# A vision state-space block with attention: the low half of the projected rows, formed by TensorE in the bank and copied by ScalarE

## The reference

```
x_hw = xc.reshape(Bsz, D, L)                       # D = 192, L = 64*64
x_wh = xc.transpose(0, 1, 3, 2).reshape(Bsz, D, L)
xs = stack([x_hw, x_wh, x_hw[..., ::-1], x_wh[..., ::-1]])   # 4 directions
x_dbl = einsum('kcd,bkdl->bkcl', x_proj_w, xs)     # 20 rows a direction
dts, Bv, Cv = split(x_dbl, [12, 16])
dt = softplus(einsum('kdr,bkrl->bkdl', dt_proj_w, dts) + dt_proj_b)
h = exp(dt * A) * h + dt * Bv * u                  # at each of 4096 positions, 4 states
y = einsum('bkdn,bkn->bkd', h, Cv)
```

## Time and profile before

| | |
|---|---|
| median of 3 runs | 10451.7 us (10447.28 to 10456.88) |
| the profiled execution, own time | 10460.32 us |
| its span | 10458.4 us |
| TensorE busy | 9132.7 us (87%) |
| VectorE busy | 7813.8 us (75%) |
| ScalarE busy | 6224.0 us (60%) |
| GpSimd busy | 3667.5 us (35%) |
| mean granted TensorE clock | 0.94 |

### The profile page before, as it was taken

The page is one execution under the profiler, slowest core; times in us unless marked ns, Lnnn a source line. Parts: engine busy times, 40 slices in busy tenths (PEclk is TensorE's granted clock), DMA queues, the critical chain, the costliest instruction groups (busy, mean ns, idle before and its releaser), DMA issues.

```text
span 10458.4 us, 108398 instructions
## 1 busy us (share of the span) xinstructions
PE 9132.7 (87%) x27904; PEld 4899.5 (47%) x27904; DVE 7813.8 (75%) x9039; ACT 6224.0 (60%) x7683; POOL 3667.5 (35%) x1920
## 2 busy tenths in 40 slices
PE   5999959999599995999959999699996999969999
PEld 2336723367233662336623366233662336623366
DVE  6977669866698666976669776697666976669776
ACT  4755647556475554755557555575555755557555
POOL 3850038500385003850048500485004850048500
PEclk8999979999799997999979999799997999979999
DMA  1320013200132001320013200132001320013200
GB/s 43 109 71 5 8 38 109 72 5 8 40 108 72 5 8 44 105 70 5 8 44 109 66 7 6 44 109 67 6 6 44 110 67 5 7 45 109 67 5 8
DMA packets 158736, 487.41 MB, mean 47 GB/s; under 512 B 21177, under 2 KB 21785, under 8 KB 125486
## 3 DMA queue, kind: packets, MB, share of 16 engines
q1 hardware_dynamic: 158254, 482.04, 14.6%
HBM read 454.69 MB, written 27.26 MB: 46 GB/s over the span
## 4 chain that ended last, share of the span: by engine, by line
PE 59%; issue 16%; DVE 15%; POOL 4%; ACT 3%; DVEq 1%; DMA 0%; ACTq 0%; SPq 0%; POOLq 0%
DVE h L1039 6%; PE ps L509 5%; PE ps L522 5%; PE ps L510 5%; PE ps L524 5%; PE ps L523 5%; PE ps L511 5%; PE ps L432 4%; PE ps L355 3%; PE ps L393 2%; PE ps L390 2%; PE ps L377 2%; PE ps L374 2%; PE ps L347 2%; PE ps L348 2%
## 5 line engine op out<-in xcount | busy, mean ns | idle before, releaser
L1164 DVE TENSOR_TENSOR pl<-pf,ph 128x1024 fp32r<-128x1024 f32 x1024 | 1254.7, 1225 | 1205.2 <-ACT ph L823 1204.1
L1039 DVE TENSOR_TENSOR_SCAN h<-ps,h,dbu 128x512 f32<-128x512 f32 x1536 | 1884.4, 1268 | 17.7 <-DVE h L1065 5.2
L897 POOL TENSOR_TENSOR dbu<-bs,du 128x1024 f32<-128x1024 f32 x768 | 1799.8, 2373 | 52.8 <-POOL du L888 52.8
L823 ACT ACTIVATE ph<-pf 128x1024 fp32r<-128x1024 f32 x1024 | 1085.3, 1060 | 833.5 <-PE ps L524 833.3
L842 POOL MEMSET xb<- 64x1024 f32 x16 | 15.2, 947 | 4280.2 <-issue 4276.5
L815 ACT ACTIVATE pf<-ps 128x1024 f32<-128x1024 f32 x1024 | 1051.0, 1026 | 644.6 <-PE ps L511 644.6
L697 ACT ACTIVATE ps<-dt,negA 128x512 f32<-128x512 f32 x1536 | 1032.6, 683 | 440.4 <-DVE h L1039 406.3
L1148 DVE TENSOR_REDUCE mx<-ps 128x1 f32<-128x512 f32 x1792 | 1164.8, 683 | 68.7 <-PE ps L432 42.2
L1047 DVE TENSOR_TENSOR hc<-h,ps 128x1024 f32<-128x1024 f32 x768 | 937.8, 1221 | 194.3 <-PE ps L366 114.5
L888 POOL TENSOR_TENSOR du<-dt,u 128x512 f32<-128x512 f32 x512 | 707.5, 1404 | 625.8 <-DVE dt L1029 625.8
L522 PE MATMUL ps<-ph,gth 128*97 128x512 f32 x2048 | 817.7, 399 | 80.8 <-ACT yraw L803 72.1
(11 more groups left out here) (175 smaller groups left out, 15899.1 us busy)
## 6 DMA issues: line engine op xcount, KB each, us to landing
bs<-rows SPq DMA_DIRECT2D x256, 1024.0 KB, 5.1
bs<-rows SPq DMA_DIRECT2D x512, 256.0 KB, 6.1
xa<-in_x SPq DMA_DIRECT2D x128, 256.0 KB, 2.9
xb<-in_x SPq DMA_DIRECT2D x128, 128.0 KB, 3.0
out<-fa SPq DMA_DIRECT2D x64, 256.0 KB, 2.0
out<-fa SPq DMA_DIRECT2D x64, 128.0 KB, 2.3
rows<-xd SPq DMA_DIRECT2D x256, 8.0 KB
gate<-in_sel SPq DMA_DIRECT2D x1, 384.0 KB
```

The source lines that it names most:

```text
L823: A(ph[:, mp % 2, :, :], pf[:, mp % 2, :, :], ACT.Copy).then_inc(S["ph_ready"], 1)
L897: pool.tensor_tensor(dbu[:, q, :, :], bs[par][:, q, :, :], du[:, r:r + 1, :].to_broadcast([P, 2, T]), ALU.mult).then_inc(S["dbu_ready"], 1)
L1039: dve.tensor_tensor_scan(h[:, j, ::step], ps[:, 2 + e, ::step], dbu[:, q, e, ::step], h[:, j, end:end + 1], ALU.mult, ALU.add)\
L1164: TT(pl[:, mp % 2, :, :], pf[:, mp % 2, :, :], ph[:, mp % 2, :, :].bitcast(F32), ALU.subtract)\
```

## The change

VectorE's `low_half` goes. TensorE gets `less_high`: a product of `minus` (minus the identity in rows 0 to 31, columns 32 to 63, zero elsewhere) with `xhl`, in fp32r, added onto bank 0 without clearing it. So partitions 32 to 63 of bank 0 then hold the rows minus their rounded value. ScalarE gets `copy_low`, which copies these 32 partitions to `xhl` and raises `xlo_ready`. `minus` is set up once, by a memset on GpSimd and one small VectorE instruction.

```
+                def less_high(par, g):
+                    pe.wait_ge(S["xhi_ready"], g + 1)
+                    mm(ps[:, 0, :], minus[:, :], xhl[par][:, :], start=False, stop=True, skip_group_check=True)\
+                        .then_inc(S["low_ready"], 1)
...
# TensorE, body
                     spread(2, par, g)
                     sum_second(g)
+                    if after:
+                        less_high(par, g + 2)
                     if nxt:
                         spread(0, 1 - par, g + 1)
# TensorE, ahead of the chunks
                 dtproj(0, g_0)
+                less_high(0, g_0)
                 spread(0, 0, g_0)
                 xdbl(0, 1, g_0 + 1)
                 dtproj(0, g_0 + 1)
+                less_high(1, g_0 + 1)
...
+                def copy_low(par, g):
+                    act.wait_ge(S["low_ready"], g + 1)
+                    A(xhl[par][LO:2 * LO, :], ps[LO:2 * LO, 0, :], ACT.Copy).then_inc(S["xlo_ready"], 1)
...
# ScalarE, body
                         soft_log(par, g + 2)
+                        copy_low(par, g + 2)
# ScalarE, ahead of the chunks
                 copy_high(0, g_0)
+                copy_low(0, g_0)
                 soft_abs(g_0)
...
                 soft_log(1, g_0 + 1)
+                copy_low(1, g_0 + 1)
...
+            TS(minus[0:LO, LO:2 * LO], eye[0:LO, 0:LO], -1.0, None, ALU.mult)
...
-                def low_half(par, g):
-                    dve.wait_ge(S["xhi_ready"], g + 1)
-                    TT(xhl[par][LO:LO + 32, :], ps[LO:LO + 32, 0, :], xhl[par][LO:LO + 32, :].bitcast(F32),
-                       ALU.subtract).then_inc(S["xlo_ready"], 1)
...
# VectorE, body
                     if after:
-                        low_half(par, g + 2)
                         residue(g + 2)
```

More of the change, by code:

```diff
@@ L88, in build @@
         eye1 = sb("eye1", [P, P])
+        minus = sb("minus", [P, P], F32R)
         avg = sb("avg", [P, P])
@@ L185, in build @@
             "conv_link", "conv_ready", "cs_ready", "u_ready",
-            "xdbl_ready", "xd_ready", "xhi_ready", "xlo_ready", "dtpre_ready", "soft_ready", "res_ready", "sp_ready",
+            "xdbl_ready", "xd_ready", "xhi_ready", "low_ready", "xlo_ready", "dtpre_ready", "soft_ready", "res_ready", "sp_ready",
             "dt_ready", "du_ready", "dA_ready", "rows_saved", "b_loaded0", "b_loaded1", "cbc_ready", "dbu_ready", "scan_link",
@@ L260, in _ @@
         def _(sp):
-            sp.wait_ge(S["pads_set"], 10)
+            sp.wait_ge(S["pads_set"], 11)
             for dst, src in LOADS:
@@ L832, in _ @@
         def _(pool):
-            for t in (win1[:, :], wo1[:, :], wa1[:, :], wx0[:, :], wx1[:, :], wdt[:, :], foldw[:, :], skip1[:, :], eye1[:, :], selr[:, :].bitcast(F32)):
+            for t in (win1[:, :], wo1[:, :], wa1[:, :], wx0[:, :], wx1[:, :], wdt[:, :], foldw[:, :], skip1[:, :], eye1[:, :], selr[:, :].bitcast(F32), minus[:, :].bitcast(F32)):
                 pool.memset(t, 0.0).then_inc(S["pads_set"], 1)
@@ L1013, in _ @@
                 dve.sem_inc(S["scan_set"], 1)
[L1015 to L1018, removed]
                 def residue(g):
@@ L1068, in _ @@
                 g_0 = b * G
-                low_half(0, g_0)
                 residue(g_0)
                 softplus(0, g_0)
-                low_half(1, g_0 + 1)
                 residue(g_0 + 1)
```

## The result

The changed kernel takes 10562.03 us in the median of 4 runs (10560.89 to 10562.93), the kernel before 10451.52 (10447.28 to 10456.88, 4 runs): a ratio of 1.0105 with an interval of 1.0088 to 1.0123. It is slower by 110.5 us where 77 was forecast; 10562 lies 8 us above the range. The profiled executions took 10562.34 and 10460.32, a difference of 102.0.

A forecast was written before the change was run, and what follows sets the result against it. VectorE bounds row-order chunks (97% busy); column-order ones are a cycle of 13.2 us TensorE and a 2.18 VectorE tail. Terms 7.65 + 0.7 + 0.95 + 0.35 = 9.65 us an item, 77 for 8: 10529, range 10498 to 10554.

The forecast's parts named there:

- Moved, and this decides: the release of the x projection: Column order: copy_low stands behind ScalarE's soft_one and log, so the x projection comes at 405.41 for 404.54: +0.87 a chunk.
- The product on TensorE is hidden: Added product behind sum_second: 0.44 us at most, done by about 404.5, before copy_low can start at 404.79.
- The mixture of gains and losses by kind of chunk: Chunks 1 to 5 -1.65 us, 6 to 8 +1.80, 9 to 13 +4.35, 14 to 16 -0.51, 17 to 28 +3.66.
- step 3: Mixed chunks with plain x projection: 14 and 15 at 14.57 us, 16 at 14.12; stretch 43.77 to 43.26.
- Step 1: Column order on ScalarE: copy_low starts 0.95 us behind the log's start, at 404.79, and ends at 405.37.
- Step 2: TensorE's granted clock: 1.00, the upper level of 2.4 GHz, in all five stretches, so no term hangs on it.
- the price of the strided products: TensorE: a product with strided moving side costs 1.96 - 1.12 = 0.84 us more; two in a column-order x projection.
- The ends: Outside chunks 1 to 28, per item: +0.7 us ahead of the chunks, +0.95 in chunk 0, +0.35 after the last x projection.
- The step from profile to median: Whole kernel: profiled execution 10460.3 lies 8.6 us above the median 10451.7, so 10537 becomes 10529.
- (a): Rival: copy hidden, VectorE's time comes back; row-order chunks 13.65 us, column-order 15.38, total 10371; chance 0.05.
- (b): Rival: column-order chunks lose less, 15.72 us by the second way round, +0.34 for +0.87; total 10485; chance 0.10.
- (c): Rival: ScalarE's copy costs more; 0.33 over the price gives 10603, the decay's price (+0.11) 10554; chance 0.10.

The follow-up runs named there:

- the release alone: Kernel before, low_half kept on VectorE, but the x projection released by a one-element ScalarE instruction behind the log: 10487.4 us, ratio 1.0037.
- ScalarE's time alone: Kernel before plus one unrelated 32 x 512 ScalarE copy that nothing waits for, behind the log: 10503.98 us, ratio 1.0049.
- the kernel with products twice: Changed kernel with each product of spread(0) issued twice, while TensorE waits for the copy: 10560.75 us, ratio 1.0104 against the kernel before.
- the kernel over 64 rows: Changed kernel with copy_low writing partitions 0 to 63 in place of 32 to 63: 10534.39 us, ratio 1.0079 against the kernel before.
- the spare copies: Kernel before plus an unrelated ScalarE copy from partition 64: 32 rows behind the log 10503.98 us, behind add_y0 10455.46; 64 rows behind add_y0 10451.56.

## Why the prediction was right in direction and too small

**The mechanism held.** "Moved, and this decides: the release of the x projection": the release alone costs a column-order chunk 0.47 (15.85), ScalarE's time alone nothing (15.38), and putting product and copy early gives 15.44. The product on TensorE is hidden, with 0.61 to spare. The copy itself takes 0.59 (0.58 taken) and holds ScalarE 0.50 (0.48 taken). The mixture of gains and losses by kind of chunk came as forecast, once the copy begins at partition 0, but for chunks 14 to 16 (step 3).

**Step 1 that failed: "log 403.84, `copy_low` 403.84 + 0.95".** It assumed that the copy overlaps the log's end as the 64-row copy in the earlier trace rows overlaps its neighbours. A copy that begins at partition 32 doesn't: 1.07. That is 0.12 a chunk, and 0.23 in chunks 14 to 16, where `add_y0` is late as well: 3.9 us in the first item, from the kernel with products twice (425.18) to the kernel over 64 rows without its two falls (423.28 - 2.04 = 421.24). The run over 64 rows gave back 27.6 us in all. The Trainium skill, "ScalarE: Activation LUTs", What ACT_TABLE_LOAD costs, gives an overlap of about 93 ns for instructions back to back and names no exception; the run over 64 rows agrees (1.05 - 0.95 = 0.10), the changed kernel doesn't (-0.02).

**Step 2: "The granted clock is 1.00 in all five ... so no term below hangs on it".** True of the kernel before, and a wrong inference. The change itself puts 0.45 to 1.10 us of idle time in one piece ahead of each x projection, and the clock falls for 3.4 us, three or four times a scan: 2.1 us in the first item by the run that keeps TensorE busy. That the idle time brings the falls is shown by this run, in which shorter waits leave one fall in eight scans, and by the release alone, whose waits are 0.46 and less from chunk 2 on and which has none. What the falls cost the whole kernel no run shows: without them the total was the same (10560.75).

**Step 3: chunks 14 to 16 at 14.57, 14.57 and 14.12.** These were worked out from the cycle through `copy_low` only. `add_y0` behind the copy was named as waiting, and priced after the last x projection alone. Here it ends a second cycle. In chunk 14 of the changed kernel it runs from 443.57 to 444.63 (above), and then:

```profile
444.68 1.97 PE L397 MATMUL ps<-pad,eye 128*128 128x512 f32 x2 [0.29 <-ACT pad L717]
```

TensorE waits another 0.29, behind the 0.77 already lost. Chunks 14 and 15 took 15.21, chunk 16 14.70. The kernel with the copy's start mended still has 44.43 in this stretch, 1.2 over the forecast. There chunk 14 takes 14.98 for 14.57: 0.19 is this second wait, and 0.22 comes from the price of the strided products. The forecast took off 2 x 0.84 = 1.68 where the x projection is plain, but TensorE's busy time in these chunks is less by 1.46 only, in the kernel before as in the changed one.

The three make 3.9 + 2.1 + 1.2 = 7.2 us in the first item, and the other stretches, without falls and with the copy's start mended, came 0.5 below the forecast: 6.7, which is 427.27 - 420.57.

**The ends.** The forecast had +2.0 an item outside the stretches. From the first x projection to that of chunk 1 it was +0.50 in the mean (+1.06 in the first item) for 1.65: the start takes 27.85 for 25.05, and chunk 0 13.33 for 15.63. In the other stages, where nothing was changed, an item takes 1.9 us less in the mean (802.0 for 804.5 in the first). With +13.8 from the first to the last scan instruction and +0.9 ahead of them, 13.8 + 0.9 - 1.9 = 12.8, and 102.0 / 8 = 12.75. The other stages take 798.7 to 805.9 over all kernels run, and this goes with the clock: they are at the lower level for 128.9 us of an item in the mean in the kernel before, 124.8 in the changed one and 128.2 with the products twice, for 111.5 where they are shortest and for 142.1 where they are longest. Why the clock there differs is open.

**The step from profile to median.** The forecast took off 8.6 us, as the profiled execution before lay that far above its median. The changed kernel's lies 0.3 above. So 25 us of the miss are in the sum, and 8 in this step.

**The rivals.** (a), the copy hidden: not here; but VectorE's time does come back in row order once the copy stands behind the first decay (13.78 for the 13.65 of this rival). (b): no column-order chunk comes near 15.72; `copy_high` still waits for `spread(2)`. (c), the copy costs more: its lower value, 10554, is nearest to the result, and 0.12 is nearly its +0.11, but by a late start and not by a longer copy. That (c)'s number is near is luck. The range stopped at this one dearer copy, with no room for what idle time on the bounding engine brings besides, and that went the same way.

**Two sums of the prediction.** (b)'s own terms, nine chunks at 0.53 and four at 0.4, make 6.4 us an item and not 5 to 6, so 10478 in place of 10485. The terms of chunk 0 give 244.01 - 243.04 = 0.97 for 0.95. Neither moves the forecast by more than 0.2 us.

## What to carry to other kernels

Work that is taken off a busy engine gains only where that engine is the bound, and its new place decides what it costs: put it behind whatever the bound waits for, and look at every instruction queued after it, not only at the one that it releases. New idle time on the engine that is the bound can have a second price, a lower clock in the work behind it; a clock of 1.00 in the profile before says nothing about the profile after. Where engines are the bound in turn, let each version of a step run in its own stretch: here that turned +110 us into -37.

## What the runs showed of the hardware

- A ScalarE copy that begins at partition 32 or 64 doesn't overlap the end of the instruction ahead: it starts 0.02 to 0.03 us after it, with 32 rows and with 64. A copy from partition 0 starts 0.06 to 0.11 before it if the last copy, `soft_abs`, `soft_relu` or `soft_one` was from partition 0 too, and 0.02 to 0.03 after it if that one was from 32 or 64 (`add_y0` in the changed kernel, `copy_xd` behind the spare copies). The copy's own time for 512 elements a partition in one line, 0.57 to 0.63, hardly depends on the rows; `add_y0`, whose target is strided in column order, takes 1.06 there.
- The granted clock fell from the upper to the lower level for 3.4 us, three or four times a scan, where TensorE idled in one piece ahead of each x projection, 0.77 in column order and 1.10 in chunks 7, 8, 23 and 24. With 0.46 and less (the release alone) it stayed at 1.00. With products issued twice, which left waits of 0.32 and 0.65, it fell once in eight scans. In the kernel with ScalarE's time alone it fell behind idle times of 1.45. In the kernel before, with 1.65 idle a row-order chunk but in pieces, it stayed at 1.00.
- A ScalarE instruction of one element takes 0.19, and releases a product on TensorE 0.24 after its start.
